# Four window numbers in a word: 5 register loads a group instead of 20 in the destination-score stage of a GNN kernel

## The chip, the cores and the metric

The kernel runs on 1 core of one Trainium2 chip. The metric is the device time of one execution in microseconds. Engines are PE (matrix multiply; its weight loads are shown as PEld, its sequencer's own instructions as PEldq), DVE (vector), ACT (scalar), POOL (GpSimd) and SP (issues DMAs).

## The reference, cut to what matters

Four graph layers with residual and layer norm follow each other. The change lies in the first, a relational attention layer over E = 60,000 edges (sorted by destination), N = 1875 nodes, 8 relations and H = 4 heads:

```python
feat_all = jnp.einsum('ni,rhid->rnhd', inputs, conv_weights)
feat_src_e = feat_all[edge_type, edge_src]
feat_dst_e = feat_all[edge_type, edge_dst]
el = jnp.sum(feat_src_e * attn_l[edge_type], axis=-1)
er = jnp.sum(feat_dst_e * attn_r[edge_type], axis=-1)
e = jax.nn.leaky_relu(el + er, negative_slope=LEAKY_SLOPE)
m = jax.ops.segment_max(e, edge_dst, num_segments=N_NODES)
ex = jnp.exp(e - m[edge_dst])
...
h = jax.ops.segment_sum(alpha[..., None] * feat_src_e, edge_dst, num_segments=N_NODES)
```

The stage in question computes `er`: for every edge, the 4 scores of its destination node under its relation.

## The kernel before, in words

All engine programs are written out by hand, each in its own block, and wait for each other by semaphores; there is no scheduler. The first 160 us build feature rows of all nodes and relations (PE L1546, ACT L578, stored by SP), with small index work of DVE and PE placed between the feature matmuls (`between`, L1532).

Edges are cut into tiles of 128. Destinations are cut into WINS = 118 windows of 16 nodes (128 pairs of node and relation). A *step* is a tile together with one window that its edges touch; there are STEPS = 586. `WS` holds each step's window number (L935, L936). Table `OFFP` holds, for each step, window number x 12 (the first column of that window in `ERW`, the destination scores in three bf16 parts of 4 heads); it is int32, with 5 words for each `a` of 128, word `c` being that of step 128 c + a. A memset and five strided multiplications by DVE fill it (L938 to L941), just behind `WS`.

**The stage of destination scores** handles 32 groups (NG) of PG = 4 values of `a`, so of 20 steps; from the 20th group on (g >= GTAIL = 19) only 16, since the last 128 steps are not full.
- PE, `broadcast_keys` (L1564): for each of the 4 values, a matmul of 512 columns (L1575), and in the first 19 groups one of 128 columns (L1577), copies the steps' keys to all partitions. It runs one group ahead.
- ACT copies two of the four banks to SBUF (L605), and the small bank (L607); then zeroes a piece of the adjacency table (L593) and, for 5 parts in 4 groups, takes the source scores out of gathered rows (`collect`, L586).
- DVE compares the keys with the partition's number (L1041, L1045), which makes one-hot tiles `KO`; `sum_parts` (L1050) adds the three bf16 parts of the group before.
- PE, `er_group` (L1580): loads the group's 20 words of `OFFP` in registers (`offsets`, L360; L362 in the trace), waits for the compare and for the sum of two groups before, and issues 20 (16) matmuls of 12 columns (L1589), each with `ERW` at the column that its register gives. Ahead of each, one fused register instruction (ISA in the listing, FUSED_REGOPS in the trace) works out the address.
- POOL meanwhile gathers source rows by indirect DMA (L547), 3 or 4 tiles a part, into 6 places; SP stores each landed part (L418). A place is free again when ACT has collected it and SP has stored it.

Before the stage PE waits for `erw_ready`: DVE splits the scores `ERF` into three bf16 parts (L1030 to L1035), for which it first waits for PE's L1557. Behind the stage PE sums the scores by tile (L1605, L1616). Then comes the adjacency walk over 586 steps (DVE L1084, L1085, L1091; PE L1626; ACT L629), in which POOL gathers the rest; then the softmax, the row stage (PE L1687, whose addresses come from a packed table by an AND and a shift of registers, L1681 to L1688) and the other layers.

```python
offs = offsets(PE, PG * SC * g, PG * SC, 3 * H * (WINS - 1), OFFP)
pe.wait_ge(s["oht"], OPG * (g + 1))
...
ins = mm(PS[4 + g % 2][:, 3 * H * k:3 * H * (k + 1)], KO[g % 3][:, lo:lo + P],
         ERW[:, bass.ds(offs[k], 3 * H)], start=True, stop=True)
```

Of the kernel before, what the change touches and what calls it, by code (L numbers as in the profile page):

```python
# [24 lines left out]
I32 = mybir.dt.int32  # L25
SP, DVE, PE = mybir.EngineType.SP, mybir.EngineType.DVE, mybir.EngineType.PE
U16 = mybir.dt.uint16
ALU = mybir.AluOpType
# [6 lines left out]
P = 128  # L35
# [3 lines left out]
H = 4  # L39
# [7 lines left out]
WINS = -(-N // WIN)  # L47
NW = WINS * WIN
STEPS = E // P + WINS
# [5 lines left out]
Q = 4 * P  # L55

FW = D + H
PG = 4
NG = P // PG
OPG = PG // 2 + 1  # L60
AU = 32
AS = 8
A_N = (STEPS - AS) // AU
TABS_AT = 10
NFS = 8
SC = -(-STEPS // P)
# [30 lines left out]
OPACK = 2 ** 15  # L97
assert STEPS % 2 == 0 and AU % 2 == 0 and KW * WINS < OPACK
RBLK = -(-TILES // RB)
# [47 lines left out]
A_HB = A_AL + H * Q  # L147
assert A_SK + 2 * AU <= A_ERS and GB * FW <= GR * STEPS
assert A_TB % LINE == 0 and A_OR + ORING * RG * P <= A_TB and RSTEPS <= Q
# [18 lines left out]
def build(nc, rec, x, xT, edge0, w0, a0l, a0r, cols, hrow, wrel, brow, wih, w1, w2, w3, b3, wp1, bp1, wl1, bl1, wr1, wp2, bp2, wl2, bl2, wr2,  # L168
          wt3, a3l, a3r, out):
    ctx = ExitStack()  # L170
    with ctx:
# [53 lines left out]
        EARLY = ADJ[:, :, :].rearrange("p r k -> p (r k)").bitcast(F32)  # L225
# [6 lines left out]
        TMP = EARLY[:, 16 * Q:20 * Q]  # L232
# [26 lines left out]
        SLO, KEY, DJ, IDX, WS, IOT = (ar(o, STEPS) for o in (A_SLO, A_KEY, A_DJ, A_IDX, A_WS, A_IOT))  # L259
# [12 lines left out]
        DG = EARLY[:, 43 * Q:44 * Q]  # L272
        LKEY = EARLY[:, 44 * Q:44 * Q + GR * (P + 1)].rearrange("p (g e) -> p g e", g=GR)
        KEY16 = EARLY[:, 47 * Q:47 * Q + SC * P // 2].bitcast(F16).rearrange("p (c e) -> p c e", e=P)
        OFFP = EARLY[:, 45 * Q + 8:45 * Q + 8 + P * SC].bitcast(I32)
        ERF = EARLY[:, 48 * Q:48 * Q + WINS * H].rearrange("p (w h) -> p w h", h=H)
        ERG = EARLY[:, 49 * Q:49 * Q + WINS * H].rearrange("p (w h) -> p w h", h=H)
        OHS = [AR[:, A_OH + k * (P // 2 + KW):A_OH + k * (P // 2 + KW) + P // 2].bitcast(F16) for k in range(AS)]
# [9 lines left out]
        ERW = AR[:, A_ERW:A_ERS].bitcast(BF16)  # L288
# [8 lines left out]
        FB, FBf = ar(A_FB, RRING, FW), ar(A_FB, RRING * FW)  # L297
        SK = ar(A_SK, 2, AU)
        SLO_KEY = ar(A_SLO, 2, STRIDE)
# [51 lines left out]
        s = {n: sem(n) for n in names}  # L351
# [8 lines left out]
        def offsets(engine, step, n, most, table=OFF):  # L360

            return nc.values_load_multi_w_load_instructions(  # L362
                table[0:1, bass.ds(step, n)],
                engines=[engine], min_val=0, max_val=most,
                skip_runtime_bounds_check_because="window and tile numbers of the walk stay in range for any sorted edges")[1]
# [196 lines left out]
        def _(act):  # L562
# [62 lines left out]
            def a_evac(i, st):  # L625


                act.wait_ge(s["a_mm"], i * AU + (st + 1))
                a.activation(EV[st % AS].rearrange("p r k -> p (r k)"), PS[4 + st % 4][:, 0:R2 * KW], ACT.Copy)\  # L629
# [5 lines left out]
            for n in range(A_N):  # L635
                for u in range(AU):
                    a_evac(n, AS + u)
# [156 lines left out]
        def _(dve):  # L794
            v = nc.vector
            chain = [0]

            def link(ins):

                chain[0] += 1  # L800
                ins.then_inc(s["dve_link"], 1)
                dve.wait_ge(s["dve_link"], chain[0])
# [132 lines left out]
            v.tensor_scalar(WS[:, 0:512], PS[5][:, :], 1.0, None, ALU.subtract)  # L935
            v.tensor_scalar(WS[:, 512:STEPS], PS[6][:, 0:STEPS - 512], 1.0, None, ALU.subtract)  # L936
            link(v.tensor_scalar(WSR, PS[7][:, 0:RSTEPS], 1.0, None, ALU.subtract))
            link(v.memset(OFFP, 0))  # L938
            for c in range(SC):
                n = min(P, STEPS - P * c)  # L940
                v.tensor_scalar(OFFP.rearrange("p (a c) -> p a c", c=SC)[:, 0:n, c], WS[:, P * c:P * c + n], float(3 * H), None, ALU.mult)  # L941
            link(v.tensor_tensor(TMP[:, 1024:1024 + STEPS], IOT, WS, ALU.subtract))
            for g in range(GR):
                v.tensor_scalar(SEL[:, g, :], TMP[:, 1024:1024 + STEPS], pcol[:, g:g + 1], None, ALU.is_equal)
# [32 lines left out]
            for c in range(SC):  # L977
                n = min(P, STEPS - P * c)
# [37 lines left out]
            def rest_of_links(k):  # L1016
# [4 lines left out]
                else:  # L1021
                    row = (NB, NL)[k - 1]
                    link(v.tensor_scalar(row, row, -1.0, BIG, ALU.add, ALU.mult))

            dve.wait_ge(s["er_ld"], 16)
            for k in range(NFS):
                dve.wait_ge(row_dma[k], fs_all[k])
# [34 lines left out]
            for c in range(SC):  # L1062
                n = min(P, STEPS - P * c)
# [36 lines left out]
            with dve.Fori(0, A_N) as i:  # L1100
                offs = pair_offsets(i * (AU // 2), AU)
# [7 lines left out]
            offs = pair_offsets(A_N * AU // 2, STEPS - A_N * AU)  # L1109
# [142 lines left out]
            for q, (t0, t1) in enumerate(GROUPS):  # L1252
                for k in (2 * q, 2 * q + 1):
                    n = min(2, NT - 2 * k)
# [149 lines left out]
            for q, (t0, t1) in enumerate(GROUPS):  # L1404
                n = t1 - t0
# [37 lines left out]
        def _(pe):  # L1443
# [95 lines left out]
            for i in range(4 * NT):  # L1539
                if i in between:  # L1540
                    between[i]()
                t, c = i // 4, i % 4
                if i >= 4:
                    pe.wait_ge(s["feat_ev"], i - 3)
                for k in range(2):
                    ins = mm(PS[c][:, :], XT0[:, k, P * t:P * (t + 1)], W0[:, k, 512 * c:512 * (c + 1)],  # L1546
                             start=(k == 0), stop=(k == 1))
# [16 lines left out]
            def broadcast_keys(g):  # L1564

                for j in range(PG):
                    if g and j < PG // 2:
                        pe.wait_ge(s["oht"], OPG * (g - 1) + j + 1)
                    elif g:
# [8 lines left out]
                    ins.then_inc(s["kb_mm"], 1)  # L1578

            def er_group(g):  # L1580
                offs = offsets(PE, PG * SC * g, PG * SC, 3 * H * (WINS - 1), OFFP)
                pe.wait_ge(s["oht"], OPG * (g + 1))
                if g >= 2:
                    pe.wait_ge(s["er_red"], g - 1)
                for j in range(PG):
                    for c in range(SC if g < GTAIL else SFULL):
                        k = SC * j + c
                        lo = 512 * j + P * c if c < SFULL else 512 * PG + P * j
                        ins = mm(PS[4 + g % 2][:, 3 * H * k:3 * H * (k + 1)], KO[g % 3][:, lo:lo + P],  # L1589
                                 ERW[:, bass.ds(offs[k], 3 * H)], start=True, stop=True)  # L1590
                ins.then_inc(s["er_mm"], 1)

            broadcast_keys(0)
# [15 lines left out]
            for c in range(SC):  # L1609
                if c + 1 < SC:  # L1610
                    step_transposes(c + 1)
                n = min(P, STEPS - P * c)
# [25 lines left out]
            for g in range(GR):  # L1638
                if g == G_EARLY:
                    pe.wait_ge(s["collected"], NPB)  # L1640
                for h in range(H):
                    ins = mm(PS[g][:, P * h:P * (h + 1)], SUM[:, P * g:P * (g + 1), h], ident[:, :],
                             start=False, stop=(h == H - 1))
# [80 lines left out]
            for i in range(R2 * NC):  # L1724
# [6 lines left out]
                for j in range(3):  # L1731
                    mm(PS[4 + j][:, 0:D], ones16[0:3, :], BP[0:3, r, :], start=True, stop=False)
                    for k in range(2):
                        ins = mm(PS[4 + j][:, 0:D], HC[i % 2][:, k, P * j:P * (j + 1)], WREL[:, k, r, :],  # L1734
                                 start=False, stop=(k == 1))
# [175 lines left out]
```

## Time and profile before

| | us |
|---|---|
| median of 3 runs (lowest, highest) | 1990.26 (1989.02, 1994.25) |
| span of the profiled execution | 1946.7 |
| median less span | 43.6 |
| busy: PE, DVE, ACT, POOL | 1461.8, 1153.3, 786.8, 531.3 |
| chain that ended last: PE, DVE, issue | 38%, 15%, 6% of the span |

The span is the time from the first to the last instruction of one execution under the hardware profiler. Matmuls are pipelined and their ends modelled, so PE's busy time is not time at its peak. "issue" as a releaser means that the engine waited for nothing that the profile shows; "remote" that the releaser isn't known. Register instructions, waits and branches are not counted as busy time. Idle time of an engine that nobody waits for costs nothing.

### The profile page before, as it was taken

The numbers are of one execution on the slowest core, as the hardware profiler recorded it, in microseconds if no ns is written. First come the engines' busy times: TensorE is split into PE (matmuls) and PEld (weight loads), VectorE is DVE, ScalarE is ACT, GpSimd is POOL, SyncE is SP. The second block draws the span as 40 slices with busy tenths as digits, with TensorE's granted clock in tenths as the row PEclk, the third lists the DMA queues.
The fourth block names the chain that finished last, engine by engine and source line by source line (L and its number), as shares of the span: only waits on it lengthen the run. The fifth ranks groups of instructions, "written<-read, shape, count | busy, mean of one in ns | idle before, by whom it ended". The sixth has DMA issues, their size and how long they took to land.

```text
span 1946.7 us, 22362 instructions
## 1 busy us (share of the span) xinstructions
PE 1461.8 (75%) x5398; PEld 733.7 (38%) x5398; DVE 1153.3 (59%) x3024; ACT 786.8 (40%) x1243; POOL 531.3 (27%) x517
## 2 busy tenths in 40 slices
PE   5894765577666766666359999798999889989930
PEld 3342433231111111111237777554445444644620
DVE  5412432239888988898999999852181460450636
ACT  1331332237666766676200000035774527327121
POOL 0105555556757666775000000000000000000023
PEclk9996555575555555555559999899999989999975
DMA  3535455554545455554129888300000010000022
GB/s 149 166 141 170 143 164 166 173 162 142 177 150 177 150 166 170 173 172 151 44 84 307 270 271 269 96 1 24 1 1 1 0 33 1 1 11 1 1 61 63
DMA packets 84509, 223.94 MB, mean 115 GB/s; under 512 B 18456, under 2 KB 27588, under 8 KB 83908
## 3 DMA queue, kind: packets, MB, share of 16 engines
q1 hardware_dynamic: 60452, 158.01, 23.4%
q0 software_dynamic: 23968, 64.77, 12.6%
q8 instruction: 53, 0.87, 0.2%
q14 instruction: 36, 0.29, 0.0%
HBM read 140.09 MB, written 82.63 MB: 114 GB/s over the span
## 4 chain that ended last, share of the span: by engine, by line
PE 38%; DVE 15%; issue 6%; DVEq 2%; ACT 1%; DMA 1%; POOL 0%; another core or an unknown queue 0%; SPq 0%; POOLq 0%
PE bank L1750 15%; PE bank L1687 11%; PE bank L1770 2%; DVE arena L1126 2%; DVE arena L1084 2%; PE bank L1734 2%; DVE adjacency L1091 2%; PE bank L1709 1%; DVE arena L1085 1%; PE bank L1839 1%; PE bank L1836 1%; PE bank L1816 1%; DVE arena L1276 1%; DVE arena L1274 1%; DVE arena L1172 1%
## 5 line engine op out<-in xcount | busy, mean ns | idle before, releaser
L547 POOL DMA_INDIRECT arena<-feat_table,arena x469 | 494.5, 1054 | 365.6 <-issue 231.4
L1626 PE MATMUL bank<-arena 128*128 128x480 f16 x586 | 337.2, 577 | 165.9 <-DVE arena L1085 96.7
L629 ACT ACTIVATE arena<-bank 128x480 uint16<-128x480 f32 x586 | 332.6, 572 | 164.4 <-PE bank L1626 109.4
L1750 PE MATMUL bank<-arena 128*128 128x472 f16 x1440 | 291.4, 366 | 10.5 <-DVE arena L1276 6.5
L555 POOL DMA_INDIRECT arena<-al_table,edge_ends x15 | 14.3, 956 | 964.7 <-DMA al_table<-arena 960.4
L1091 DVE TENSOR_TENSOR adjacency<-adjacency,arena 128x480 uint16 x586 | 234.3, 400 | 38.8 <-issue 22.8
L1687 PE MATMUL bank<-arena 128*128 x966 | 229.5, 392 | 0.8 <-issue 0.3
L1626 PEld LDWEIGHTS bank<-arena 128*128 128x128 f16 x586 | 60.9, 104 | 442.4 <-issue 219.9
L1750 PEld LDWEIGHTS bank<-arena 128*128 128x128 bf16 x1440 | 141.8, 99 | 160.2 <-issue 12.4
L1085 DVE TENSOR_SCALAR arena<-iota,arena 128x480 f16<-128x480 f16 x586 | 199.0, 340 | 0.0
L1687 PEld LDWEIGHTS bank<-arena 128*128 128x128 f32 x966 | 174.0, 190 | 56.6 <-issue 35.3
L1182 DVE TENSOR_TENSOR arena<-arena 128x1024 f32<-128x1024 f32 x118 | 140.3, 1213 | 16.9 <-DMA arena<-edge_rows 15.2
L1084 DVE TENSOR_SCALAR arena<-iota,arena 128x128 f16<-128x128 f16 x586 | 145.4, 248 | 4.1 <-ACT adjacency L593 4.1
L722 ACT ACTIVATE arena<-adjacency 128x1888 f16<-128x1888 uint16 x30 | 108.8, 3633 | 45.9 <-PE bank L1750 45.9
L703 ACT ACTIVATE arena<-adjacency 128x1888 f16<-128x1888 uint16 x30 | 109.0, 3636 | 33.7 <-PE bank L1750 33.7
L1589 PE MATMUL bank<-arena 128*128 x588 | 75.9, 187 | 53.3 <-issue 47.7
L1546 PE MATMUL bank<-arena 128*128 128x512 f32 x240 | 111.4, 620 | 5.9 <-ACT arena L578 3.0
L605 ACT ACTIVATE arena<-bank 128x512 f16<-128x512 f32 x64 | 35.3, 597 | 173.6 <-remote 81.1
L1575 PE MATMUL bank<-adjacency,ident 128*128 128x512 f16 x128 | 67.4, 617 | 47.1 <-DVE arena L1041 35.5
L661 ACT ACT_TABLE_LOAD x2 | 2.6, 1283 | 239.8 <-DVE ln_mean_var L1228 239.8
L1297 DVE COPY arena<-bank 128x472 f32<-128x472 f32 x12 | 7.0, 642 | 143.4 <-PE bank L1750 143.3
L1589 PEld LDWEIGHTS bank<-arena 128*128 128x128 f16 x588 | 58.6, 105 | 86.4 <-issue 74.7
(289 smaller groups left out, 1544.6 us busy)
## 6 DMA issues: line engine op xcount, KB each, us to landing
arena<-edge_rows SPq DMA_DIRECT2D x117, 520.0 KB, 4.7
edge_rows<-arena SPq DMA_DIRECT2D x67, 520.0 KB
edge_rows<-arena SPq DMA_DIRECT2D x67, 390.0 KB
feat_table<-arena SPq DMA_DIRECT2D x60, 260.0 KB, 2.1
arena<-feat_table,arena POOLq DMA_INDIRECT x469
arena<-in_w SPq DMA_DIRECT2D x1, 2048.0 KB, 10.1
arena<-in_xT SPq DMA_DIRECT2D x1, 1920.0 KB, 18.3
arena<-in_x SPq DMA_DIRECT2D x1, 1792.0 KB
```

The source lines that it names most:

```text
L547: g.indirect_dma_start(out=PLACE[k][:, t - lo, :], out_offset=None, in_=feat_t, in_offset=bass.IndirectOffsetOnAxis(ap=IE[:, t:t + 1], axi ...
L629: a.activation(EV[st % AS].rearrange("p r k -> p (r k)"), PS[4 + st % 4][:, 0:R2 * KW], ACT.Copy)\
L703: a.activation(chunk(CH1, c % 2, wide), ADJ[:, r, :].rearrange("p (n s) -> p n s", s=SH)[:, :, sh], ACT.Copy).then_inc(s["chunk_ready"], 1)
L1084: v.tensor_scalar(OHS[st % AS], iota128[:, :], lo, None, ALU.is_equal)
L1085: v.tensor_scalar(OHK[st % AS], iota480[:, :], key, None, ALU.is_equal).then_inc(s["a_oh"], 1)
L1091: v.tensor_tensor(dst, dst, EV[st % AS], ALU.add).then_inc(s["a_add"], 1)
L1182: v.tensor_tensor(rows, rows, al, ALU.mult).then_inc(s["r_wgt"], 1)
L1546: ins = mm(PS[c][:, :], XT0[:, k, P * t:P * (t + 1)], W0[:, k, 512 * c:512 * (c + 1)], start=(k == 0), stop=(k == 1))
L1589: ins = mm(PS[4 + g % 2][:, 3 * H * k:3 * H * (k + 1)], KO[g % 3][:, lo:lo + P], ERW[:, bass.ds(offs[k], 3 * H)], start=True, stop=True)
L1626: mm(PS[4 + st % 4][:, 0:R2 * KW], OHS[st % AS], OHK[st % AS], start=True, stop=True).then_inc(s["a_mm"], 1)
L1687: mm(BANKS[:, bass.ds(out_at, D)], OHR[:, (st // RG) % ORING, P * (st % RG):P * (st % RG + 1)], FBf[:, bass.ds(places[st % RK] >> 12, D)], ...
L1750: ins = mm(PS[4 * fo + j][:, 0:CW], m[:, P * fo:P * (fo + 1)], ch[:, CW * j:CW * (j + 1)], start=(c == 0 and q == 0), stop=(c == n - 1 and ...
```

## The change

The table holds the window number itself (7 bits) instead of its column, and four of them, for the 4 values of a group, in one word: `OFFP` has 32 x 5 words. PE loads 5 words for a group. Ahead of each matmul it shifts the word (not for the first of the four), masks 7 bits, and multiplies by 12. The table is made by nine linked instructions of DVE further down, behind L1014 and `rest_of_links`: the window numbers are cast to int32 in the scratch region `TMP`, then three times shifted and ORed.

```diff
+WBITS = 7
+WFULL = 2 ** WBITS
...
-        OFFP = EARLY[:, 45 * Q + 8:45 * Q + 8 + P * SC].bitcast(I32)
+        OFFW = TMP[:, 0:P * SC].bitcast(I32).rearrange("p (c g j) -> p c g j", c=SC, j=PG)
+        OFFP, OFFT = (EARLY[:, 45 * Q + 8 + NG * SC * k:45 * Q + 8 + NG * SC * (k + 1)].bitcast(I32) for k in range(2))
...
-            link(v.memset(OFFP, 0))
-            for c in range(SC):
-                n = min(P, STEPS - P * c)
-                v.tensor_scalar(OFFP.rearrange("p (a c) -> p a c", c=SC)[:, 0:n, c], WS[:, P * c:P * c + n], float(3 * H), None, ALU.mult)
...
+            OFFF = OFFW.rearrange("p c g j -> p (c g j)")
+            link(v.memset(OFFF, 0))
+            link(v.tensor_copy(OFFF[:, 0:STEPS], WS))
+            OPv = OFFP.rearrange("p (g c) -> p c g", c=SC)
+            OTv = OFFT.rearrange("p (g c) -> p c g", c=SC)
+            link(v.tensor_copy(OPv, OFFW[:, :, :, 0]))
+            for j in range(1, PG):
+                link(v.tensor_single_scalar(OTv, OFFW[:, :, :, j], WBITS * j, ALU.logical_shift_left))
+                link(v.tensor_tensor(OFFP, OFFP, OFFT, ALU.bitwise_or))
...
-                offs = offsets(PE, PG * SC * g, PG * SC, 3 * H * (WINS - 1), OFFP)
+                words = offsets(PE, SC * g, SC, WFULL ** PG - 1, OFFP)
...
+                        off = nc.s_assert_within((words[c] >> (WBITS * j) & (WFULL - 1)) * (3 * H), 0, 3 * H * (WINS - 1),
+                                                 skip_runtime_bounds_check_because="a window's number times the width of its scores")
                         ins = mm(PS[4 + g % 2][:, 3 * H * k:3 * H * (k + 1)], KO[g % 3][:, lo:lo + P],
-                                 ERW[:, bass.ds(offs[k], 3 * H)], start=True, stop=True)
+                                 ERW[:, bass.ds(off, 3 * H)], start=True, stop=True)
```

How PE's instructions stand in the first group of the stage, from the register load on, in the kernel before (L362 is the load, L1589 the small matmul, ISA its fused register instruction):

```order
L362 TENSOR_LOAD adjacency
L1589 ISA
L1589 MATMUL bank<-arena 128x12
L1589 ISA
L1589 MATMUL bank<-arena 128x12
```

And in the changed kernel (the load is L365, the matmul L1599), its first matmul and then the fifth and the sixth, where the shift begins:

```order
L365 TENSOR_LOAD adjacency
L1599 REGISTER_ALU
L1599 ISA
L1599 MATMUL bank<-arena 128x12
...
L1599 REGISTER_ALU
L1599 ISA
L1599 MATMUL bank<-arena 128x12
L1599 REGISTER_ALU x2
L1599 ISA
L1599 MATMUL bank<-arena 128x12
```

One register instruction has come in ahead of each of the first 5 matmuls of a group and two ahead of each of the others; the number of loads is the same.

On DVE, ahead of the stage, in the kernel before:

```order
L1013 TENSOR_TENSOR arena<-adjacency,arena 4x512
L1014 TENSOR_SCALAR arena<-arena 4x512
L1030 CAST unsorted_flag<-bank 128x1
L1031 CAST arena<-adjacency 128x118x4
```

And in the changed kernel:

```order
L1012 TENSOR_TENSOR arena<-adjacency,arena 4x512
L1013 TENSOR_SCALAR arena<-arena 4x512
L1025 MEMSET adjacency 128x640
L1026 CAST adjacency<-arena 128x586
L1029 COPY adjacency<-adjacency 128x5x32
L1031 TENSOR_SCALAR adjacency<-adjacency 128x5x32
L1032 TENSOR_TENSOR adjacency<-adjacency 128x160
...
L1038 CAST unsorted_flag<-bank 128x1
L1039 CAST arena<-adjacency 128x118x4
```

The nine instructions (the pair of L1031 and L1032 stands three times) now lie between the last flag and the splitting of the scores.

## Rows read from the trace of the kernel before

**Rows 1.** The head of the page.

```profile
span 1946.7 us, 22362 instructions
```

**Rows 2.** Stretches: us, busy time of each engine (instructions), PEclk, DMA share, GB/s.

```profile
163.00:405.00 242.00, 141.95 (x792) 80.44 (x792) 75.26 (x132) 69.45 (x153) 142.81 (x150) 0.51 0.53 167
440.00:930.00 490.00, 330.08 (x571) 59.23 (x570) 430.99 (x1728) 334.40 (x661) 329.79 (x297) 0.50 0.51 162
...
173.00:193.00 20.00, 3.26 (x24) 1.94 (x21) 1.16 (x2) 0.00 (x0) 12.55 (x14) 0.50 0.65 206
193.00:206.00 13.00, 11.45 (x67) 6.65 (x65) 6.74 (x12) 7.15 (x16) 6.62 (x7) 0.50 0.40 121
```

(The engines stand in the order PE, PEld, DVE, ACT, POOL.)

**Rows 3.** Groups of instructions, 163 to 410 us: busy, mean ns, idle before, releasers.

```profile
L1589 PE MATMUL bank<-arena 128*128 x588 | 75.9, 187 | 53.3 <-issue 47.7 <-DVE arena L1041 3.1 <-DVE arena L1050 1.1
```

**Rows 4.** Waits of POOL, 163:405 and 440:930: us in total, times, longest.

```profile
POOL arena L547 <- ACT arena L586: 56.5, 17, 6.8
...
POOL arena L547 <- ACT arena L586: 69.8, 30, 9.8
```

**Rows 5.** PE in order of time: start, us, count [idle before <-releaser].

```profile
79.99 1.17 PE L1502 MATMUL bank<-adjacency 128*128 128x512 f16 x8 [3.05 <-DVE adjacency L947]
...
195.97 2.65 PE L1589 MATMUL bank<-arena 128*128 x20 [0.21 <-DVE arena L1050]
...
200.65 2.17 PE L1589 MATMUL bank<-arena 128*128 x20
...
209.14 0.24 PE L1589 MATMUL bank<-arena 128*128 x3 [1.19 <-issue]
...
347.94 2.12 PE L1589 MATMUL bank<-arena 128*128 x16 [1.01 <-DVE arena L1041]
...
351.66 2.09 PE L1589 MATMUL bank<-arena 128*128 x16
```

**Rows 6.** POOL in order of time.

```profile
187.32 0.95 POOL L547 DMA_INDIRECT arena<-feat_table,arena  x1 [0.30 <-issue]
188.57 0.95 POOL L547 DMA_INDIRECT arena<-feat_table,arena  x1 [0.30 <-issue]
196.31 0.94 POOL L547 DMA_INDIRECT arena<-feat_table,arena  x1 [6.79 <-ACT arena L586]
```

**Rows 7.** Line 362: duration ns min/median/max, first and last start us.

```profile
L362 PEldq TENSOR_LOAD <-arena x121: 330/333/783, 1010.9 to 1244.4; - x121
L362 PEldq TENSOR_LOAD <-adjacency x32: 1227/1365/2531, 166.7 to 398.0; - x32
```

(Those from `adjacency` load 20 registers, those from `arena` the row stage's 4.)

**Rows 8.** Line 1687 in 1014.1 to 1015.55 us, four steps.

```profile
L1687 PEldq FUSED_REGOPS  x8: 42/62/83, 1014.2 to 1015.5; - x8
L1687 PEldq ALU_OP  x4: 32/32/32, 1014.3 to 1015.4; - x4
```

**Rows 9.** PEld in order of time, the first group.

```profile
168.28 2.51 PEld L1589 LDWEIGHTS bank<-arena 128*128 128x128 f16 x20 [0.90 <-issue]
```

**Rows 10.** Line 1589, whole execution.

```profile
L1589 PEldq FUSED_REGOPS  x588: 2/46/1396, 168.2 to 403.6; - x196
```

**Rows 11.** DVE in order of time.

```profile
73.42 0.59 DVE L938 MEMSET adjacency<- 128x640 int32 x1 [0.20 <-DVE adjacency L937]
...
74.70 0.77 DVE L942 TENSOR_TENSOR adjacency<-arena 128x586 f32<-128x586 f32 x1
...
156.07 0.26 DVE L1006 TENSOR_TENSOR scores<-scores,iota 1x110 int32<-1x110 int32 x1
...
160.88 0.16 DVE L1030 CAST unsorted_flag<-bank 128x1 int32<-128x1 f32 x1 [0.77 <-PE bank L1557]
```

**Rows 12.** Line 941.

```profile
L941 DVE TENSOR_SCALAR adjacency<-arena x5: 228/278/284, 74.0 to 74.6; 128x128 int32<-128x128 f32 x4, 128x74 int32<-128x74 f32 x1
```

**Rows 13.** Groups of instructions of DVE, 420 to 425 us.

```profile
L1069 DVE TENSOR_TENSOR arena<-arena 128x293 int32<-128x293 int32 x1 | 0.5, 466 | 0.0
L1067 DVE TENSOR_SCALAR arena<-arena 128x586 int32<-128x586 f32 x1 | 0.5, 455 | 0.0
```

## The prediction

> **What bounds the kernel now.** I read the head of the page and the table of stretches first [rows 1, 2]. They show a span of 1946.7 us in stages with different limits. The change touches one of them, the stretch from 163 to 405 us, in which PE multiplies one-hot tiles by windows of destination scores. In those 242 us PE is busy for 142, DVE for 75, ACT for 69 and POOL for 143, so no engine's busy time explains the stage. The three runs have a median of 1990.26 us, 43.6 us more than the span; I take that difference as fixed. A difference of under 0.3% (6 us) can't be told from none here.
>
> Next the groups of instructions of the stage [rows 3]. It holds 588 of the small matmuls (19 groups of 20, 13 of 16: 380 + 208), and PE's idle time before them is "issue" in 47.7 of 53.3 us: PE's array waits for its own sequencer, not for another engine. POOL gathers beside it (150 gathers), and its longest kind of wait there is for ACT to take the scores out of a landed part, 56.5 us in all [rows 4].
>
> Then the order of time on PE [rows 5]. Two kinds of stretch alternate. In the first, groups follow each other: the matmuls of one start at 195.97, of the next at 200.65 (4.7 us later), and with 16 matmuls at 347.94 and 351.66 (3.7 us). In the second, the same matmuls come by ones to threes with 0.5 to 1.2 us between them, and PE is then held up for several us more. The table of stretches shows that it isn't PE alone: between 173 and 193 us DVE is busy for 1.2 us and ACT not at all, while POOL goes on gathering; between 193 and 206 us all of them work [rows 2]. In my count along this timeline 22 of the 32 groups ran through at the quick pace (13 of the large, 9 of the small); the rest fell into about ten slow stretches. What makes all sequencers slow there the views don't name. A slow stretch ends when POOL has run out of places (it stops after 188.57 and resumes at 196.31, the 6.79 us before it put down to ACT), and one begins some 10 us after POOL resumes: at 207 here [rows 5, 6].
>
> **The register load.** A load of 20 registers takes 1.365 us on PE's sequencer, one of 4 takes 0.333 us [rows 7]; that is 0.0645 us a register, so 5 take about 0.40 us, and the change saves 0.96 us a group, 32 x 0.96 = 31 us. At the quick pace most of this is exposed: the load stands between the last matmul that was sent and the next group's first. The Trainium skill, "Runtime: NRT & Kernel Launch", section "Instruction fetch mechanics", gives about 200 ns a register for such loads. By that, 15 fewer would save 3.0 us a group and 96 us in all. The trace says a third of it for loads from SBUF.
>
> **The added register instructions.** The listing of the two programs shows one REGISTER_ALU more ahead of each of the first 5 matmuls of a group and two more ahead of the others: 5 + 15 x 2 = 35 in a group of 20, 4 + 12 x 2 = 28 in one of 16, so 19 x 35 + 13 x 28 = 1029. What does one cost PE's sequencer? From below: its own duration is 0.032 us at the reader of the row table, which uses the same operations [rows 8]. From above: there 4 steps with 12 register instructions fill 1.45 us, 0.36 us a step, where a step of the small matmuls (one register instruction, one weight load, one matmul) takes 2.51 / 20 = 0.125 us [rows 8, 9]. Two more register instructions are thus 0.24 us, 0.12 each; but one of the two at L1687 is a fused one of 62 ns in the median, 30 ns longer than a plain one. I take 0.095 us, nearer to the upper row because that row contains the turnaround of the sequencer and the lower doesn't. That is 3.3 us for a large group and 2.7 for a small one, 98 us in all (33 to 123).
>
> Net of the load, a group at the quick pace grows by 2.35 us (4.7 becomes about 7.0) or by 1.7 us (3.7 becomes 5.4). The fused instruction also does a multiplication more; that is inside the bounds.
>
> **What of it is exposed.** At the quick pace PE's sequencer is what everyone waits for: DVE's sums wait for the matmuls, and ACT's copies for the broadcasts ahead of them. I charge the 22 quick groups in full: 13 x 2.35 + 9 x 1.7 = 46 us. The ten groups in slow stretches I charge with nothing, since there every engine is late already (in full they would add 21 us). Something comes back. The stage now holds 133 us of quick pace (19 x 4.5 + 13 x 3.7, all groups; 4.5 is the rounded mean of the large ones), and, in the 236 us from its first load at 166.7 to its last matmul at 403 [rows 7, 10], 236 - 133 = 103 us of slow stretches and waits. These go with POOL's gathering. POOL needs 150 x 1.25 = 188 us for it (the distance of two gathers) [rows 6], 80% of 236; over 282 us it is 67%. If the slow time falls in that proportion, 103 becomes 86, and 17 us come back. Stage: 46 - 17 = +29 us.
>
> **The table's preparation.** Removed: a memset and five strided multiplications on DVE at 73.4 us, together 1.28 us from the memset's start to the next instruction's [rows 11]. They lie ahead of L947, for which PE waits 3.05 us [rows 5], and PE's run of feature matmuls behind it is unbroken: -1.3 us. Added, behind L1014: nine linked instructions. The memset is 0.59 us, the cast of 586 elements 0.46 (L1067), the strided copy and three shifts 0.28 each (0.278 for 128 strided elements at L941), three ORs 0.33 each (between 0.26 for 110 at L1006 and 0.47 for 293 at L1069): 3.2 us [rows 11 to 13]. Behind them on DVE are queued the flag's copy and the splitting of the scores, and PE's first broadcast waits for that. The 0.77 us for which DVE waits for PE at L1030 cover a part: +2.4 us [rows 11]. If that cover were gone, it would be 3.2. Together +1.1 us. POOL's gathers began before this and don't wait for it, so ACT finds more parts landed; nothing waits there.
>
> **Behind the stage** the start of the adjacency walk waits for PE's score matmuls and ACT's zeroing; the walk itself is DVE's, busy for 431 of 490 us [rows 2], and POOL has 69.8 us of waits for ACT in it [rows 4]. So an end of the stage later by x moves everything by x; no later cover takes it up.
>
> **Sum:** 1946.7 + 29 + 1.1 = 1977 us of span, and with the 43.6 us around it **2020 us**, 1.5% above the median.
>
> **Rivals.**
> *The slow stretches dissolve (faster).* Now PE runs three groups quickly, gives POOL many places at once, and POOL gathers on end; a slow stretch follows some 10 us after. With groups of 7.0 and 5.4 us PE frees places more slowly than POOL fills them (1.25 parts a group, 4.4 gathers of 1.25 us, 5.5 us), so POOL would gather with short pauses. In the walk its busy share is higher (330 of 490 us against 143 of 242) and yet DVE is busy for 88% of it: steady gathering alone doesn't make the engines slow [rows 2]. It gives a gain once more than 67 of the 103 us are gone (then the 67 us of all groups' growth are covered). PE's sequencer then sets the stage, 133 + 67 = 200 us, with some 10 us of leftovers 210: -26 us, 1965 us. Against it: the slow stretches come while stores and gathers overlap, and both remain. Chance 0.22.
> *Register instructions are nearly free.* At 0.032 us each they cost 33 us where the load saves 31, and only two thirds of either is exposed: +2 us with the preparation, 1992 us. For it is the row of their own duration; against it the step of 0.36 us at L1687. The same page and section of the Trainium skill as above puts the sequencers' floor at about 20 cycles an instruction; no run here shows so little for PE, whose three instructions of a step take 0.125 us. Chance 0.11.
> *All of it shows.* Slow stretches are as long as before and the groups in them grow as well: 67 us + 1, 2058 us. For it: more instructions have to pass a sequencer that is already stalling, and a fused one took up to 1.396 us there [rows 10]. Chance 0.12.
> *The words don't shorten the load.* The listing shows one load a group in both programs, of 5 words now; nothing speaks for this one, and I give it no chance of its own.
>
> **Chances and range.** My case, with +8 to +50 us, has 0.55. Slower by over 0.3%: 0.55 + 0.12 = 0.67. Faster: 0.22 and 0.03 of the second rival, 0.25. Same: the other 0.08. The range reaches from 1960, which holds the first rival's value and a little more, to 2050, 10 us beyond my own case's upper end; outside lie the third rival and a part of the first, about 2 in 10. The slower cases alone would give 1998 to 2055.
>
> **What would show it.** Right: a load median near 0.40 us, 35 and 28 more register instructions a group, matmuls of a quick group over about 6 us instead of 2.2 to 2.8 with "issue" before them, DVE's sums waiting for them, the first broadcast 1 us later, the stage at about 270 us, and the walk and all behind it shifted and unchanged. PE's granted clock, 0.50 in the stretches of rows 2, stays there. Wrong: quick groups under 5 us (the price of a register instruction), or quick groups of 7 us and a stage of 200 to 215 us with DVE and ACT busy throughout (the slow stretches). A walk longer or shorter by over 5 us would refute that the rest only moves.

## The result, and the profile after

The changed kernel took 2045.14 us (median of 4 runs, 2039.93 to 2048.18), the kernel before 1992.26 us beside it: ratio 1.026 (95% interval 1.023 to 1.030), 53 us longer. The forecast was 2020 us, in a range of 1960 to 2050.

The head of the changed kernel's page, the two stretches of [rows 2] (here the second one still holds the last 21 us of the stage, and ends before the walk does; PE, PEld, DVE, ACT, POOL, then PEclk, DMA share, GB/s):

```profile
span 2041.9 us, 23395 instructions
...
163.00:405.00 242.00, 130.68 (x650) 67.34 (x648) 62.57 (x106) 58.23 (x128) 114.88 (x121) 0.51 0.43 133
...
440.00:930.00 490.00, 312.81 (x604) 67.81 (x603) 377.77 (x1482) 294.07 (x580) 299.21 (x278) 0.52 0.49 152
```

By 405 us PE had sent 650 matmuls of the stage's stretch where it had sent 792 before, and POOL had issued 121 gathers for 150. The stage had not ended. The small matmul's line and the load's line over the whole execution (answers to [rows 3, 7, 10]):

```profile
L1599 PEldq ALU_OP  x1029: 2/36/737, 166.2 to 461.3; - x172
L1599 PEldq FUSED_REGOPS  x588: 2/55/721, 166.3 to 461.4; - x196
L1599 PE MATMUL bank<-arena x588: 167/188/216, 166.5 to 461.5; 128*128 x196
its engine sat idle before it (us, times) until:
  issue: 278.5, 634
...
L365 PEldq TENSOR_LOAD <-adjacency x32: 584/1232/2043, 165.1 to 455.1; - x32
```

The 1029 register instructions are there. From the first load to the start of the last small matmul the stage lasts 296 us (165.1 to 461.5), where it was 236 (166.7 to 402.9). A load of 5 registers has a median of 1.23 us, against 1.365 for 20: the saving that the change is built on is almost absent.

Ahead of the stage, PE's wait of 3.05 us at L1502 [rows 5] has shrunk (the line is L1510 now):

```profile
74.73 1.17 PE L1510 MATMUL bank<-adjacency 128*128 128x512 f16 x8 [1.62 <-DVE adjacency L946]
```

PE in order of time, a quick group of the changed kernel (the row "x20" of 2.2 to 2.65 us in [rows 5] answers to it):

```profile
190.80 0.63 PE L1583 MATMUL bank<-adjacency,ident 128*128 128x512 f16 x1
191.23 0.31 PE L1585 MATMUL bank<-adjacency,ident 128*128 128x128 f16 x1
191.33 1.32 PE L1599 MATMUL bank<-arena 128*128 x7
192.84 1.17 PE L1599 MATMUL bank<-arena 128*128 x4 [0.18 <-issue]
194.20 1.17 PE L1599 MATMUL bank<-arena 128*128 x4 [0.19 <-issue]
195.59 1.17 PE L1599 MATMUL bank<-arena 128*128 x4 [0.23 <-issue]
196.95 0.19 PE L1599 MATMUL bank<-arena 128*128 x1 [0.18 <-issue]
...
199.16 1.31 PE L1599 MATMUL bank<-arena 128*128 x7
```

The next group starts 7.8 us later (191.33 to 199.16), 3.1 more than the 4.7 of [rows 5]; small groups take 6.5. So quick groups run on at the pace of PE's sequencer. But each fourth group (0, 4, 8 and so on) is a slow stretch of 12 to 15 us, the first one of 24. Here is the inside of such a group:

```profile
214.80 1.00 PE L1599 MATMUL bank<-arena 128*128 x8
216.89 0.17 PE L1599 MATMUL bank<-arena 128*128 x1 [1.09 <-issue]
218.38 0.19 PE L1599 MATMUL bank<-arena 128*128 x1 [1.31 <-issue]
```

POOL's order of time shows what each fourth group has of its own. ACT takes 5 parts in 4 groups, and the two of one group come just ahead of PE's fourth (here at 208.75 us). POOL then gathers on end, ten times from 209.73 to 220.97, where ahead of the other groups it gathers three or four times and then waits for ACT:

```profile
202.03 0.94 POOL L550 DMA_INDIRECT arena<-feat_table,arena  x1 [4.41 <-ACT arena L589]
...
209.73 0.94 POOL L550 DMA_INDIRECT arena<-feat_table,arena  x1 [3.01 <-ACT arena L589]
...
220.97 0.94 POOL L550 DMA_INDIRECT arena<-feat_table,arena  x1 [0.30 <-issue]
231.22 0.94 POOL L550 DMA_INDIRECT arena<-feat_table,arena  x1 [9.31 <-ACT arena L589]
```

### The profile page after: what moved, and what is told of

Same layout as the page of the kernel before. It is cut to its first block, busy times and chain, and to the rows that moved or that the text cites. A ratio compares the mean times of both kernels' runs of the same rounds, so it can differ in the third digit from the quotient of the medians.

```text
span 2041.9 us, 23395 instructions
## 1 busy us (share of the span) xinstructions
PE 1492.2 (73%) x5398; PEld 742.1 (36%) x5398; DVE 1160.8 (57%) x3027; ACT 786.6 (39%) x1243; POOL 524.9 (26%) x517
## 4 chain that ended last, share of the span: by engine, by line
PE 38%; DVE 10%; issue 2%; ACT 1%; DMA 1%; POOL 0%; DVEq 0%; SPq 0%; another core or an unknown queue 0%; POOLq 0%
PE bank L1760 14%; PE bank L1697 11%; PE bank L1780 2%; DVE arena L1134 2%; PE bank L1744 2%; PE bank L1719 1%; PE bank L1849 1%; PE bank L1846 1%; PE bank L1817 1%; PE bank L1826 1%; DVE arena L1180 1%; PE bank L1805 1%; DVE arena L1284 1%; DVE arena L1282 1%; DVE ln_stats L1229 0%
## 5 line engine op out<-in xcount | busy, mean ns | idle before, releaser
L550 POOL DMA_INDIRECT arena<-feat_table,arena x469 | 488.1, 1041 | 454.1 <-issue 228.3
L1697 PE MATMUL bank<-arena 128*128 x966 | 229.5, 392 | 0.7 <-issue 0.3
L1599 PE MATMUL bank<-arena 128*128 x588 | 102.6, 188 | 136.5 <-issue 90.7
L1092 DVE TENSOR_SCALAR arena<-iota,arena 128x128 f16<-128x128 f16 x586 | 144.9, 247 | 1.2 <-ACT adjacency L596 1.2
L1599 PEld LDWEIGHTS bank<-arena 128*128 128x128 f16 x588 | 59.6, 107 | 193.8 <-issue 187.9
L1058 DVE TENSOR_REDUCE arena<-bank 128x80 f32<-128x240 f32 x32 | 13.0, 407 | 184.7 <-PE bank L1599 173.8
```

Source lines behind the costliest of these rows:

```text
L550: g.indirect_dma_start(out=PLACE[k][:, t - lo, :], out_offset=None, in_=feat_t, in_offset=bass.IndirectOffsetOnAxis(ap=IE[:, t:t + 1], axi ...
L1092: v.tensor_scalar(OHS[st % AS], iota128[:, :], lo, None, ALU.is_equal)
L1697: mm(BANKS[:, bass.ds(out_at, D)], OHR[:, (st // RG) % ORING, P * (st % RG):P * (st % RG + 1)], FBf[:, bass.ds(places[st % RK] >> 12, D)], ...
```

## The experiments

The chips differ: beside some of the runs the kernel before took 1955 us, beside others 1990. Times below are therefore told as ratios to before on the same chip. On one chip the runs of before lie within some 20 us of each other (1944 to 1965 for 17 of them), so a few us between two single traces mean nothing. "Stage" is the time from the first register load to the start of the last small matmul, "walk" that between the first and the last start of its line L1084 (L1092 and so on in the others), each in one profiled execution, so that stages of kernels compared with each other can come from different chips.

| kernel | ratio to before (95%) | before there, us | stage | walk |
|---|---|---|---|---|
| before, again | 0.998 (0.996 to 1.001) | 1955 | 237 | 515 |
| changed, again | 1.027 (1.024 to 1.029) | 1955 | 291 | 519 |
| load_of_five | 1.001 (0.997 to 1.005) | 1955 | 234 | 512 |
| alu_only | 1.034 (1.030 to 1.038) | 1955 | 301 | 515 |
| aligned_five | 1.022 (1.019 to 1.025) | 1955 | 280 | 509 |
| twenty_shifted | 1.021 (1.017 to 1.025) | 1955 | 274 | 515 |
| no_gathers_in_stage | 1.045 (1.039 to 1.050) | 1955 | 144 | 509 |
| after_no_gathers | one run, 2179 us | 1990 | 240 | 539 |
| one_part_a_group | 1.000 (0.997 to 1.003) | 1955 | 205 | 547 |
| spaced_one | 1.003 (1.001 to 1.006) | 1990 | 241 | 546 |
| spaced_three | 0.983 (0.979 to 0.987) | 1990 | 207 | 535 |
| changed_spaced_three | 0.986 (0.982 to 0.990) | 1990 | 233 | 506 |

**Both kernels again.**

> The kernel before, unchanged, profiled once more. The first profile had a span of 1946.7 us beside runs of 1989 to 2000 us; the changed kernel's profile has a span of 2041.9 us beside 2043.59 us for the same execution. Theory 1 (the first profile of before was an execution of its own, shorter than the timed ones): a span of 1986 to 1998 us here, 1 to 2 us under its time, with the 40 us found in the walk of the adjacency or behind it. Theory 2 (about 43 us lie outside the span): again 1946 us beside 1990 us.

The span was 1952.0 us beside a time of 1953.70 for the same execution: 1.7 us lie outside, not 43.6. Theory 1 holds in kind. Its numbers, 1986 to 1998, don't, since this chip was one of the quicker. The trace of before that I read probably belongs to such a chip (its span is 1946.7), and the median beside it to a slower one; the record doesn't name the two chips.

> The changed kernel, unchanged, on the chip and beside the runs of before that the following three share. Its ratio to before should be the one measured (1.023 to 1.030), or, if the register instructions weigh the same 59 us of stage everywhere and this chip is the one with before at 1955 us, 1.03. In the stage: 24 of the 32 loads of 5 words take 1.23 us and the 8 of the groups 0, 4, 8 ... take 0.59 us.

Ratio 1.027, the same as the first time; stage 291 us, 54 us more than before's 237, and 56 us of time (2011.4 against 1955.08 us for before). The walk is 519 us here, 4 us more than before's on a chip of the same pace. The first trace of the changed kernel had 534, and spaced_one, which does next to nothing and ran on a slower chip, 546. So the 30 us between the walks of the first two traces go for the most part with chip and execution, not with the change.

**The two halves of the change apart.**

```diff
-                offs = offsets(PE, PG * SC * g, PG * SC, 3 * H * (WINS - 1), OFFP)
+                offs = offsets(PE, PG * SC * g, SC, (3 * H - 1) * (WINS - 1), OFFP)
...
-                                 ERW[:, bass.ds(offs[k], 3 * H)], start=True, stop=True)
+                                 ERW[:, bass.ds(offs[c] + j, 3 * H)], start=True, stop=True)
```

(and 11 for 12 as the table's factor, so that the columns stay inside the window table)

> The load alone: PE loads 5 words a group and not 20, every matmul keeps its one fused register instruction and no other is added. Left out: the right columns (the 4 values of a group share 5 words, so the scores are not the reference's). Theory H (the load is hidden behind the 4 to 8 broadcast matmuls that PE's array still works through): quick groups stay at 4.2 to 4.8 and 3.7 us, the stage and the time within 4 us of before. Theory E (exposed, as predicted): quick groups shorter by 0.96 us each, 21 to 31 us less in all.

PE in order of time, two groups of this kernel that follow each other, and the load's line:

```profile
284.36 2.08 PE L1589 MATMUL bank<-arena 128*128 x20
...
288.46 1.52 PE L1589 MATMUL bank<-arena 128*128 x20
...
L362 PEldq TENSOR_LOAD <-adjacency x32: 578/582/1495, 167.3 to 398.5; - x32
```

Neither theory holds whole. The load took 0.58 us and quick groups became shorter by 0.8 us: the next load comes 3.5 us later for 4.3, and 2.95 for 3.7 in small groups. (In the rows above the matmuls of the two groups start 4.1 us apart, for 4.7 in [rows 5].) So H, the cover by the broadcasts, is refuted. Yet the stage was 234 us and the time the same: what quick groups gave up, the slow stretches took. In the kernel before, a shorter quick group buys nothing.

```diff
+                        off = nc.s_assert_within((offs[k] >> (7 * j) & 63) * (3 * H), 0, 3 * H * (WINS - 1),
+                                                 skip_runtime_bounds_check_because="at most 63 x 12")
...
-                                 ERW[:, bass.ds(offs[k], 3 * H)], start=True, stop=True)
+                                 ERW[:, bass.ds(off, 3 * H)], start=True, stop=True)
```

> The register instructions alone: 20 words are loaded as before, and each matmul gets the shift, the mask and the multiplication. Left out: the right columns (the mask is applied to the unpacked column numbers). If 0.1 us for each of the 1029 added instructions is the whole loss, quick groups have 5.8 and 5.0 us of matmuls and the time equals that of the changed kernel (2045 us) within 4 us by theory H (the load's size doesn't matter), or is 21 to 31 us above it by theory E.

Ratio 1.034 against the changed kernel's 1.027: the register instructions are the whole loss, and the shorter load takes 0.7% back (11 to 13 us), less than theory E's 21 to 31. Quick groups take 7.9 and 6.6 us, 3.6 and 2.9 more than before (4.3 and 3.7): 3.6 / 35 and 2.9 / 28 make 0.10 us an instruction.

**Why five words took 1.23 us.** In the changed kernel 24 loads take about 1.23 us and those of groups 0, 4, 8 and so on 0.59; in load_of_five 27 of 32 take 0.58 (the other five, up to 1.5 us, are those of the first two groups and some in slow stretches). The changed kernel's words begin at 20 g bytes from the table's start, load_of_five's at 80 g.

```diff
-        OFFP, OFFT = (EARLY[:, 45 * Q + 8 + NG * SC * k:45 * Q + 8 + NG * SC * (k + 1)].bitcast(I32) for k in range(2))
+        OFFP, OFFT = (EARLY[:, 45 * Q + 8 + NG * 8 * k:45 * Q + 8 + NG * 8 * (k + 1)].bitcast(I32) for k in range(2))
...
-                words = offsets(PE, SC * g, SC, WFULL ** PG - 1, OFFP)
+                words = offsets(PE, 8 * g, SC, WFULL ** PG - 1, OFFP)
```

> The changed kernel with 8 words of table a group of which 5 are used, so that each group's 5 words begin at a multiple of 32 bytes from the table's start. Theory A (a register load's time depends on where its words begin: 0.58 us at a multiple of 16 bytes, 1.23 us elsewhere): all 32 loads take 0.58 us, the 24 groups that had 1.23 us get shorter by up to 0.65 us, 15 us in all. Theory B (the 1.23 us are the place in the rhythm of four groups, as the slow group is every fourth too): loads stay as in the changed kernel. Should the loads be shorter and the groups not, the load lies behind the broadcast matmuls.

The opposite test moves the old table of 20 words a group by one word:

```diff
-        OFFP = EARLY[:, 45 * Q + 8:45 * Q + 8 + P * SC].bitcast(I32)
+        OFFP = EARLY[:, 45 * Q + 9:45 * Q + 9 + P * SC].bitcast(I32)
```

> The kernel before with its table moved by one word, so that each group's 20 words begin 4 bytes behind the old places; nothing else changes. Theory A: a load goes in pieces of 4 words where it can (20 words in 5 pieces, 1.36 us) and word by word, at about 0.25 us, where it can't: 20 x 0.25 = 5 us a load. Theory B: 1.36 us as before.

The load's line in the changed kernel again, in aligned_five, and in twenty_shifted:

```profile
L365 PEldq TENSOR_LOAD <-adjacency x32: 583/1235/1954, 164.6 to 448.8; - x32
```

```profile
L365 PEldq TENSOR_LOAD <-adjacency x32: 430/582/1354, 165.6 to 438.9; - x32
```

```profile
L362 PEldq TENSOR_LOAD <-adjacency x32: 4733/5470/6552, 166.3 to 432.6; - x32
```

Theory A holds both ways. Aligned, loads take 0.58 us, quick groups 7.1 instead of 7.8, and the stage is 11 us shorter (280 for 291; 24 x 0.65 = 16 was the bound), the ratio 1.022 for 1.027. Shifted by 4 bytes, 20 words take 5.47 us and the time rises by 2.1%, with no instruction changed. The durations fit pieces of up to 4 words at about 0.25 us each: 4 words 0.33, 5 aligned ones 0.58, 20 aligned ones 1.36, 5 unaligned ones 1.23 (5 x 0.25). The Trainium skill, "Runtime: NRT & Kernel Launch", section "Instruction fetch mechanics", has about 200 ns a register for a TENSOR_LOAD: near the unaligned ones here (0.25 us), and three times too much for 20 aligned ones (1.36 / 20 = 0.068 us). The slow fourth groups stay in aligned_five, so they don't come from the addresses.

**What the slow stretches are.**

```diff
-                for m in range(GC_UP * (g - 1) // GC_DOWN if g else 0, GC_UP * g // GC_DOWN):
-                    collect(m)
             act.wait_ge(s["er_mm"], NG)
+            for m in range(GC_ER):
+                collect(m)
```

> The kernel before, in which ACT takes all 38 parts behind the stage rather than between its groups, so that POOL fills its 6 places and then gathers nothing until the stage is over. The whole becomes longer; only the stage is looked at. If the slow stretches belong to the gathers and stores beside the stage: all groups at the quick pace, the stage's first load to last matmul in 130 to 150 us. If they come from PE's own instruction supply or from something else: slow stretches remain, and the stage stays over 200 us.

> The changed kernel, in which ACT takes all 38 parts behind the stage, so that POOL gathers nothing beside it after its 6 places are full; the stage alone is looked at. Before had 144 us so. If PE's sequencer alone sets the stage then: 19 x 7.8 + 13 x 6.6 = 234 us and some us for the first groups, 90 us more than before's 144, and every group quick, the fourths too (with gathers each fourth group takes 12 to 14 us). If the slow fourth groups come from the addresses or the program itself: they stay.

The stretch of 60 us from 200 us, of before again (with gathers), of before without gathers and of the changed kernel without gathers:

```profile
200.00:260.00 60.00, 39.87 (x236) 24.01 (x236) 19.86 (x35) 21.06 (x46) 35.47 (x37) 0.50 0.53 167
```

```profile
200.00:260.00 60.00, 59.77 (x389) 38.71 (x388) 34.20 (x58) 30.98 (x55) 0.00 (x0) 0.50 0.00 1
```

```profile
200.00:260.00 60.00, 42.60 (x221) 23.06 (x221) 20.74 (x36) 18.00 (x32) 0.00 (x0) 0.50 0.00 1
```

Without gathers PE does 389 matmuls in the time for 236, and slow groups are gone in both kernels but for the first ones, in which POOL still fills its places. The stage is 144 us before and 240 changed. So the change costs PE's sequencer 96 us (by one trace of each kernel), and with gathers only 54 to 60 of them show.

```diff
-GC_UP, GC_DOWN = 5, 4
+GC_UP, GC_DOWN = 1, 1
```

> The kernel before, in which ACT takes one gathered part a group rather than 5 in 4 groups: 31 parts beside the stage, not 38, and 7 more beside the walk. With no gathers the stage was 144 us, with 38 parts 236. If the slow stretches go with the number of gathers, the stage loses (7/38) x 92 = 17 us or more, and the walk, where POOL waited 70 us for ACT, takes the 7 x 4.4 = 31 us of gathers in: 10 to 20 us faster as a whole. If the walk doesn't have that room: the gain comes back as waits of ACT for landed parts, time unchanged or longer.

Seven parts fewer make the stage 32 us shorter (205 for 237), and the walk 32 us longer (547 for 515); the time is the same. So the room in the walk isn't there, and a part costs about 4.6 us wherever it is gathered, a little more than its 3.5 gathers of 1.25 us on POOL. Waits of DVE's line of the walk, before again and in this kernel:

```profile
DVE adjacency L1091 <- issue: 23.7, 32, 1.9
```

```profile
DVE adjacency L1091 <- issue: 46.1, 51, 2.6
```

Of the 32 us that the walk grows by, 22 come back as more of the same "issue" waits, on DVE now; ACT doesn't wait for parts there.

**Gathers further apart.** POOL gets memsets of an unused tile of 8 columns ahead of each gather, one or three:

```diff
                 for t in range(lo, hi):
+                    for j in range(3):
+                        pool.wait_ge(s["fill"], 3 * t + j)
+                        g.memset(FILL[:, :], 0.0).then_inc(s["fill"], 1)
                     g.indirect_dma_start(out=PLACE[k][:, t - lo, :], out_offset=None, in_=feat_t,
```

> The kernel before with one small memset of an unused tile ahead of each of POOL's gathers, chained by a semaphore, so that gathers come about 0.2 us further apart (1.4 to 1.5 us for 1.25). If slow stretches come from a backlog (gathers at 266 KB in 1.25 us and the stores of the same bytes ask for more than the DMA engines move, and PE's instructions come late behind it): shorter slow stretches, the stage under 230 us and the time the same or up to 20 us less. If POOL's own time is what stage and walk wait for: 150 x 0.2 = 30 us longer in the stage, and more in the walk.

> As spaced_one with three memsets ahead of each gather, gathers 1.7 to 1.9 us apart. By the backlog theory the slow stretches are gone (no step of 0.7 us an instruction), and the stage lasts as long as POOL takes for 150 gathers, 255 to 285 us. By the other theory (each gather costs the other engines a fixed time, however far apart they are) the slow time stays at 90 us and comes on top.

One memset changes nothing that was meant: gathers stay 1.25 us apart, since it fits in the 0.30 us that POOL idled between two. The run is a control, 0.3% longer. Three make the distance 1.54 us. POOL in order of time, and the stage's stretch in spaced_three:

```profile
207.92 0.95 POOL L551 DMA_INDIRECT arena<-feat_table,arena  x1
208.88 0.44 POOL L550 MEMSET filler<- 128x8 f32 x3
209.46 0.95 POOL L551 DMA_INDIRECT arena<-feat_table,arena  x1
```

```profile
163.00:372.00 209.00, 141.69 (x789) 80.86 (x788) 73.12 (x133) 70.20 (x153) 174.00 (x522) 0.51 0.53 167
```

The fused register instructions, to be held against 1.396 us at most in [rows 10]:

```profile
L1593 PEldq FUSED_REGOPS  x588: 46/46/56, 166.3 to 370.5; - x196
```

The slow stretches are gone, the stage is 207 us instead of 241 (my 255 to 285 was too long: 38 parts have only 133 gathers, and the first ones were issued before it), and the time is 1.7% under before's. DMA share and GB/s over the stage are what they were before (0.53 and 167): not the mean load makes an engine's instructions late but gathers packed in bursts (the slow stretch of [rows 2], 173 to 193 us, had 206 GB/s). The 266 KB that the expectation of spaced_one gives a gather is a gather and its store together: before again moved 19.92 MB for 149 gathers in 163 to 405 us, 0.134 MB each, and 20.33 MB on the stores' queue. Every fourth group still takes 10 to 11 us in spaced_three, but not by slow instructions: PE waits for ACT, and ACT for a part. POOL now never waits for a place, and everyone waits for parts, ACT above all:

```profile
ACT arena L590 <- DMA arena<-feat_table,arena: 130.3, 34, 6.0
```

The DMA view lists a queue that it calls "instruction". In before again (163 to 405 us), in spaced_three (163 to 372) and in the kernel without gathers (190 to 308), in packets, MB and share of the 16 engines:

```profile
q8 instruction: 9, 0.15, 0.2%
```

```profile
q8 instruction: 9, 0.15, 0.3%
```

```profile
q8 instruction: 8, 0.13, 0.5%
```

By the shares that is about 1 us a packet in each (an estimate). So these packets don't themselves take longer where the instructions are late. Whether they start late isn't shown.

> The changed kernel with the three memsets ahead of each gather (gathers 1.54 us apart at least), as spaced_three did with the kernel before, whose stage then took 207 us, set by POOL's gathers, without slow stretches. If slow stretches are the backlog alone: they are gone here too, PE's sequencer sets the stage at 235 to 242 us (240 less 207 = 33 us more), POOL gets pauses again, and the time is 1.3 to 1.7% above spaced_three's, about level with the kernel before (ratio 0.995 to 1.003). If the register instructions weigh the whole 90 us of PE's time: ratio 1.03. If POOL's gathers bound stage and walk together and the stage's growth disappears in them: ratio 0.983, as spaced_three.

The line of the small matmul here, to be held against ALU_OP 2/36/737 in the changed kernel:

```profile
L1603 PEldq ALU_OP  x1029: 32/36/45, 165.9 to 397.0; - x172
L1603 PEldq FUSED_REGOPS  x588: 55/55/65, 166.0 to 397.1; - x196
```

No register instruction takes over 65 ns. PE's sequencer sets the stage at 233 us, 26 more than spaced_three's, near what the first theory said (235 to 242). But the time isn't 1.3 to 1.7% above spaced_three's. The ratios are 0.986 (0.982 to 0.990) and 0.983 (0.979 to 0.987), not to be told apart: the walk is 506 us instead of 535 and takes the 26 us back. That is the third theory. Waits of POOL from 160 to 960 us, in spaced_three and here:

```profile
POOL arena L551 <- issue: 6.5, 5, 1.5
```

```profile
POOL arena L554 <- issue: 7.6, 9, 1.5
POOL filler L553 <- issue: 4.5, 4, 1.8
```

The 469 gathers start between 155.3 and 945.2 us in spaced_three and between 152.3 and 937.6 here, 790 and 785 us, and POOL idles for 7 and 12 us of them. So with steady gathers POOL bounds stage and walk together, and PE's added time lies under its gathers.

## Why the prediction was right or wrong

- **What bounds the stage.** Right that PE's sequencer sets the quick groups and that the rest goes with POOL's gathering. I left open what makes the sequencers slow. The runs show it as an effect of gathers on end: without gathers the slow time is gone, with gathers 1.54 us apart too. By what path a burst holds back the instructions of PE, DVE and ACT isn't shown, and gathers weren't separated from the stores that follow them. A queue of transfers ahead of the instructions' own packets would be one guess; it wasn't tested, and the packets themselves take about 1 us with and without gathers.
- **The register load.** This step failed. I took 0.0645 us a register from [rows 7] and so 0.40 us for 5, a saving of 0.96 us in each of 32 groups (31 us). Measured: 1.23 us in the 24 groups whose words don't begin at a multiple of 16 bytes, 0.59 in the 8 whose words do. So against alu_only, with its 20 words, a quick group of the changed kernel is only 0.1 us shorter where the load isn't aligned, and 0.8 where it is. Both kinds of load in [rows 7] behave as aligned loads of whole fours, so a price a register drawn from them holds for no other load.
- **The register instructions.** Right: 0.095 us each forecast, 0.10 measured; 3.3 and 2.7 us a group forecast, 3.6 and 2.9 measured. The upper row, [rows 8, 9], was the right one to lean on, and the instruction's own 0.036 us would have been wrong by three times.
- **Quick pace of all groups.** I had 133 us before and 200 after. Without gathers it was 144 and 240 (some 12 us of each are the slow first groups). The growth is 96 us where I had 67. Of the 29 between them the load makes about 22 (24 x 0.1 + 8 x 0.8 = 9 us saved for 31) and the register instructions 8 (19 x 3.6 + 13 x 2.9 = 106 for 98).
- **What comes back.** I let 17 us come back of 103 slow ones and left 21 us in slow groups uncharged: 38 of 67. Of 96 us, 36 to 42 came back: my share was too large, and my amount right by luck. I charged by POOL's share of time, and the runs show something else: slow time follows bursts of gathers, and POOL has a burst at each fourth group.
- **The table's preparation.** DVE's nine instructions run from 154.94 to 158.68 + 0.33 us, 4.1 us where I had 3.2; strided ones of 160 elements take 0.44, not 0.28. PE's wait of 3.05 us at L1502 is 1.62 in the changed kernel, 1.4 less for the 1.3 that I gave. The stage's first load starts at 165.1 us, against 166.7: -1.6 us forecast as +1.1. The second pair of traces has 164.6 and 164.4. It is noise beside the rest.
- **What follows the stage.** "Moved and unchanged" holds on chips of the same pace: walk 519 us against 515. My test of it, 5 us, failed between the first two traces (534 against 504). The second pair says that this isn't the change; the test was too fine for traces of different chips.
- **The base.** I added the 43.6 us between span and median as fixed. In the runs here they are 1 to 2 us. The trace of before came from an execution some 40 us shorter than the median. Since I took them as fixed and forecast a difference, this did no harm.
- **The rivals.** "Slow stretches dissolve" came true in other kernels, and not in this one: in twenty_shifted, where PE stands in a load for 5.5 us of each 8.3, and under spaced gathers. Here the quick groups were slow enough for POOL to pause in three groups of four, and the fourth had its two parts at once. "Nearly free" is refuted by alu_only, and "all of it shows" by no gathers: 96 us would have been.

So the sum came to +30 us where 53 were measured, on the right side. The 53 lie just beyond the +8 to +50 us of my own case, in the part of the range that was added for the rivals. With what comes back about as I had it (38 us of 36 to 42), the gap is the 29 us of growth that I had too little, three quarters of it by the load.

## What to carry to other kernels

Price a register load by the address as well as by the count, and lay tables out so that each load begins at a multiple of 16 bytes (from the start of a table whose aligned loads are quick); packing that broke this, and that swapped one load of aligned words for an unpacking of each word, lost here, and still lost with the loads aligned (1.022). Price register instructions by the step between neighbours, not by their own duration. Where the trace shows every engine slow at once beside a DMA burst, look at the spacing of the transfers first: memsets worth 0.3 us a gather gave 1.7%, where a shorter load for PE in the same stage (load_of_five) gave nothing.

## What was not expected of the hardware

- A load of 20 registers takes 1.36 us at aligned words and 5.47 us when the table lies 4 bytes further on.
- While gathers come every 1.25 us beside stores, PE's register instructions take up to 0.74 us each in the changed kernel (1.40 in before) and matmuls come 0.5 to 4 us apart; at 1.54 us between gathers the same instructions never take over 65 ns, at the same 167 GB/s over the stage (before and spaced_three).
- Chips differ by 1.8% on this kernel (1955 and 1990 us). In single traces much of it lies in the walk: spaced_one, in effect the kernel before, has 546 us there on a slower chip and before has 515 on a quicker one. The gain by spacing was measured on the slower chips alone.
